# Q and K of the next batch inside the attention loop, 64x64 score matmuls with a plain maximum, and GpSimd sums cut into tiles

## The reference

```
xn = layernorm(x)
q, k, v = xn @ Wq + bq, xn @ Wk + bk, xn @ Wv + bv    # 16 heads of 16
# blocks of 64 rows; a block's queries see the 192 keys of the blocks
# before, at and behind it, within a band |i - j| <= 64 and inside the sequence
scores = where(mask, einsum(q, k) / sqrt(16), -1e9)
a = softmax(scores) @ v @ Wo + bo
h = layer_norm(a + xn) * g1 + b1
f = gelu(h @ W1 + c1) @ W2 + c2                       # 256 -> 1024 -> 256
attn = layer_norm(f + h) * g2 + b2
e = argmax(xn @ gate_w.T)                             # one expert of 8 per token
ffn = xn + xn @ expert_w[e].T
out = x + attn + ffn
```

## Time and profile before

| | us |
|---|---|
| median of 3 runs | 1558.98 |
| lowest and highest | 1557.52, 1561.96 |
| span of the profiled execution | 1553.1 |
| TensorE matmul busy | 1240.9 (80%) |
| VectorE busy | 1071.5 (69%) |
| ScalarE busy | 739.8 (48%) |
| GpSimd busy | 739.9 (48%) |

### The profile page before, as it was taken

How to read it: one execution, slowest core, us unless ns; L and a number is a source line. 1 busy time by engine, 2 the same in 40 slices (tenths; PEclk the granted TensorE clock), 3 DMA queues, 4 the chain that set the end, 5 groups by cost and what they waited for, 6 DMA issues and landing times.

```text
span 1553.1 us, 34323 instructions
## 1 busy us (share of the span) xinstructions
PE 1240.9 (80%) x10696; PEld 714.8 (46%) x10696; DVE 1071.5 (69%) x3743; ACT 739.8 (48%) x1356; POOL 739.9 (48%) x749
## 2 busy tenths in 40 slices
PE   0648885999678985999859997689858898599967
PEld 0424452735346353654527454373535535265435
DVE  8656775777757775867757677576766676587565
ACT  1305744366543744447443565426544374445642
POOL 6443745156531766037550474406752177504661
PEclk9959997999989997989979899798988899799979
DMA  7463056220733119130462206422082212912010
GB/s 237 92 139 118 3 117 122 76 92 29 144 79 100 57 69 166 50 112 13 108 131 69 99 8 145 91 83 83 33 156 75 88 57 74 162 48 94 2 28 28
DMA packets 89647, 135.00 MB, mean 87 GB/s; under 512 B 10209, under 2 KB 62305, under 8 KB 87393
## 3 DMA queue, kind: packets, MB, share of 16 engines
q1 hardware_dynamic: 83328, 115.91, 30.0%
q0 software_dynamic: 6144, 16.79, 4.4%
HBM read 74.47 MB, written 59.90 MB: 87 GB/s over the span
## 4 chain that ended last, share of the span: by engine, by line
PE 49%; DMA 17%; issue 11%; POOL 8%; DVE 8%; SPq 3%; ACT 3%; DVEq 0%; POOLq 0%; ACTq 0%
DMA pair_dram<-pool 9%; PE bank L1132 8%; PE bank L1035 8%; PE bank L1154 8%; PE bank L1036 7%; PE bank L1038 7%; PE bank L1181 6%; DMA q_s<-q_s 5%; DVE xn L604 2%; SPq L284 2%; DMA ys_dram<-xn 2%; PE bank L1102 2%; POOL x_sb L453 2%; POOL x_sb L451 2%; POOL rs L386 2%
## 5 line engine op out<-in xcount | busy, mean ns | idle before, releaser
L713 DVE CUSTOM_DVE_ANT_0 bank<-bank,mask 128x192 f32<-128x192 f32 x1024 | 337.3, 388 | 199.1 <-PE bank L1132 195.1
L943 ACT ACTIVATE pool<-bank 128x512 f32<-128x512 f32 x512 | 293.0, 597 | 118.9 <-PE bank L1154 113.2
L1132 PE MATMUL bank<-k_s,q_s 128*64 128x192 f16 x2048 | 175.3, 269 | 144.1 <-DMA q_s<-q_s 141.2
L440 POOL TENSOR_SCALAR_AFFINE_SELECT pool<-pool 128x512 f32<-128x512 f32 x256 | 172.2, 675 | 194.1 <-ACT pool L943 193.4
L1154 PE MATMUL bank<-q_s,k_s 128*128 128x256 f16 x1024 | 199.3, 290 | 28.7 <-issue 21.3
L389 POOL TENSOR_TENSOR rs<-ve,neghalf 128x1 f32<-128x1 f32 x64 | 36.9, 577 | 384.8 <-DVE ve L776 384.8
L1132 PEld LDWEIGHTS bank<-k_s,q_s 128*64 128x64 f16 x2048 | 77.8, 113 | 250.1 <-issue 226.9
L1181 PE MATMUL bank<-pool,v_a 128*32 128x256 f32 (+2 forms) x2560 | 161.1, 345 | 19.9 <-DVE pool L727 8.6
L989 ACT ACTIVATE pool<-bank,c1c 128x512 f32<-128x512 f32 x128 | 87.8, 686 | 169.5 <-PE bank L1038 132.5
L790 DVE TENSOR_TENSOR pool<-pool 128x512 f16<-128x512 f32 x128 | 106.7, 839 | 63.3 <-ACT pool L955 62.2
L713 DVE DVE_READ_ACCUMULATOR2_ANT m_sb<- 128x1 f32 x1024 | 144.6, 141 | 0.3
(11 more groups left out here) (149 smaller groups left out, 2511.1 us busy)
## 6 DMA issues: line engine op xcount, KB each, us to landing
pair_dram<-pool SPq DMA_DIRECT2D x32, 512.0 KB, 7.6
xn<-xs_dram SPq DMA_DIRECT2D x40, 384.0 KB, 3.7
ys_dram<-xn SPq DMA_DIRECT2D x120, 128.0 KB, 1.7
q_s<-pair_dram SPq DMA_DIRECT2D x48, 256.0 KB
k_s<-pair_dram SPq DMA_DIRECT2D x48, 256.0 KB
x_sb<-in_L_attn_x SPq DMA_DIRECT2D x8, 1024.0 KB, 5.7
res_dram<-x_sb SPq DMA_DIRECT2D x8, 1024.0 KB, 4.8
res_r<-res_dram SPq DMA_DIRECT2D x8, 1024.0 KB, 7.4
```

Of the source, the lines that this page charges most:

```text
L440: nc.gpsimd.affine_select(out=p, in_=p, compare_op=ALU.is_ge, fill=0.0, base=0, pattern=[[0, 4], [1, 2 * W]], channel_multiplier=-1).then_ ...
L713: ins = nc.vector.tensor_tensor_reduce(out=SB[u % 2][:, i * WIN:i * WIN + WIN], in0=SB[u % 2][:, i * WIN:i * WIN + WIN], in1=mask[:, v, :] ...
L943: nc.scalar.activation(prob[:, (k + 2) % 3, 2 * pu:2 * pu + 2, :], TB[u % 2][:, :].rearrange("p (h q) -> p h q", h=2), ACT.Exp, scale=EXP_ ...
L1132: mm = nc.tensor.matmul(SB[u % 2][W * bl:W * bl + W, i * WIN:i * WIN + WIN], q_s[:, h, W + w0:2 * W + w0], k_s[:, h // 2, w0:w0 + WIN], st ...
```

## The change

Seven things change.

- Q and K of the next batch are computed in thirds (two matmuls each) within steps 18 to 29 of the attention loop, two thirds a step, over the two banks of `MB` instead of four banks. For that the norm moves ahead: statistics in steps 0 to 8, `xn` from step 10, its transposes from step 14. x is loaded one turn earlier, within the sorted tiles of the turn before.
- The columns of Wq and Wk are permuted on the way in, so that a head's 16 channels lie eight partitions apart; stores go to `pair_dram` slot by slot (12 of 256 KB instead of 4 of 512 KB), and loads fill 48 partitions at once (8 of 384 KB instead of 12 of 256 KB and two small ones).
- Plain scores: eight matmuls of 48 rows by 64 stationary columns, heads of the two partition halves into different banks, and four matmuls with an identity that add the mask in PSUM; both halves in one block. VectorE then takes two reductions over 2 x 192 instead of four instructions with a mask and four reads.
- The maxima's transpose uses a bank of `SB`; TensorE waits for it before the next scores of that step.
- Transposed scores keep their shape; the two halves of a step are grouped by partition half and are not split by plain scores.
- VectorE's factor of the second norm moves behind two tiles of V.
- GpSimd's sums over eight tiles become eight sums of one tile each.

```
-    XN_AT = 23
+    XN_AT = T + 2
+    XT_AT = XN_AT + 4
+    QK_AT = XT_AT + 4
-        QB, VB = TB + MB, OB + TB
+        QB, VB = MB, OB + TB
...
+            def pair_stores(b, i):
+                c, qk = divmod(i, 2)
+                for src, done, slots in ((qk_h, qk_hi, (0, 2 if qk else 1)), (qk_l, qk_lo, (1 if qk else 2,))):
+                    sp.wait_ge(done.sem, done.at(b, 2 * i + 2))
+                    for slot in slots:
+                        sp.dma_start(pair_dram[c, qk, :, :, slot, :, :].rearrange("j a d s -> d (j a) s"),
+                                     src[:, 2 * qk + c, :]).then_inc(pair_st[i % 2].sem, 16)
+            def stack_loads(b, i, first=False):
+                c, qk = divmod(i, 2)
+                if not first and qk == 0:
+                    sp.wait_ge(ST_ps.sem, ST_ps.at(b - 1, 4 * T * (c + 1)))
+                sp.wait_ge(pair_st[i % 2].sem, pair_st[i % 2].at(b, 48 * (i // 2 + 1)))
+                for a in range(2):
+                    dst = k_s[:, 4 * c:4 * c + 4, :] if qk else q_s[:, 8 * c + a:8 * c + 8:2, :]
+                    sp.dma_start(dst[W * a:W * a + KW, :, W:W + S],
+                                 pair_dram[c, qk, :, a, :, :, :].rearrange("j o d s -> (o d) j s")).then_inc(stack[c].sem, 16)
...
+                    if i == 10 and x_next:                      # sorted_tiles, SP
+                        load_x(b + 1)
             def turn(b, last):                                  # SP
                 max_rows(b, 1)
-                if not last:
-                    load_x(b + 1)
                 load_res(b)
-                for g in range(2, G):
-                    max_rows(b, g)
-                if not last:
-                    store_res(b + 1)
-                    stacks(b + 1)
+                max_rows(b, 2)
+                max_rows(b, 3)
+                if not last:
+                    # pair_stores 0, 1; stack_loads 0, 1; pair_stores 2, 3; stack_loads 2, 3
+                    store_res(b + 1)
                     sorted_tiles(b + 1)
...
-                nc.gpsimd.tensor_tensor(res_r[:, :, :], res_r[:, :, :], x_sb[:, :, :], ALU.add).then_inc(res_y.sem, 1)
+                for t in range(T):
+                    nc.gpsimd.tensor_tensor(res_r[:, t, :], res_r[:, t, :], x_sb[:, t, :], ALU.add).then_inc(res_y.sem, 1)
...                                                              # likewise the other five sums
+            def qk_low(b, u):                                   # VectorE
+                dve.wait_ge(qk_hi.sem, qk_hi.at(b, u + 1))
+                nc.vector.scalar_tensor_tensor(out=qk_l[:, o, s], in0=QB[u % 2][:, :], scalar=bqk[:, o:o + 1],
+                                               in1=qk_h[:, o, s], op0=ALU.add, op1=ALU.subtract).then_inc(qk_lo.sem, 1)
...
             def c2_stage(b, first=False):                       # VectorE
-                if not first:
-                    nm1_stage(b - 1)
                 for t in range(T):
+                    if t == 2 and not first:
+                        nm1_stage(b - 1)
...
             def maxima(b, j):
+                for n, par in enumerate((1, 0)):
+                    dve.wait_ge(S_ps.sem, S_ps.at(b, 2 * j + n + 1))
-                        ins = nc.vector.tensor_tensor_reduce(
-                            out=SB[u % 2][:, i * WIN:i * WIN + WIN], in0=SB[u % 2][:, i * WIN:i * WIN + WIN], in1=mask[:, v, :], scale=1.0,
-                            scalar=-3.0e38, op0=ALU.add, op1=ALU.max, accum_out=m_sb[:, h, t:t + 1])
+                    nc.vector.tensor_reduce(m_sb[:, 4 * g + par:4 * g + 4:2, t],
+                                            SB[par][:, 0:2 * WIN].rearrange("p (h c) -> p h c", h=2), AX.X, ALU.max).then_inc(mx.sem, 1)
...
             def turn(b, last):                                  # VectorE
-                    if k == 2 * T + MAX_AT and not last:
+                    if k < T and not last:
+                        c1_tile(b + 1, k)
+                    if k == T and not last:
                         c1_stage(b + 1)
+                    if XT_AT <= k < XT_AT + 4 and not last:
+                        xn_low(b + 1, k - XT_AT)
+                    if QK_AT <= k < QK_AT + 12 and not last:
+                        for third in range(2 * (k - QK_AT), 2 * (k - QK_AT) + 2):
+                            if third % 3 == 2:
+                                qk_low(b + 1, third // 3)
...                                                              # ScalarE: qk_high at the same places
+            def qk_third(b, u, part):                           # TensorE
+                o, hf = u % 4 // 2 * 2 + u // 4, u % 2
+                dst = QB[u % 2][:, :]
+                if part == 0:
+                    if u >= 2:
+                        pe.wait_ge(qk_lo.sem, qk_lo.at(b, u - 1))
+                    else:
+                        pe.wait_ge(xT_l.sem, xT_l.at(b, 4))
+                # two matmuls of 512 columns; the third part ends with .then_inc(qk_ps.sem, 1)
+            def score_mm(out, n, j, par, i):
+                h, r = 2 * g + i, slice(W * par, W * par + KW)
+                q = W + (2 * t + n) * W
+                return nc.tensor.matmul(out[W * n:W * n + W, i * WIN:i * WIN + WIN], q_s[r, 2 * h + par, q:q + W], k_s[r, h, q - W:q + 2 * W],
+                                        start=i == 0, stop=False, skip_group_check=True)
+            def mask_mm(out, n, t, par):
+                r = slice(W * par, W * par + W)
+                band = mask[r, edge(2 * t + n), :, :].unsqueeze(1).broadcast_to([W, 2, 2, W])
+                dst = out[W * n:W * n + W, 0:2 * WIN].rearrange("p (h c k) -> p h c k", h=2, c=3)[:, :, 0::2, :]
+                return nc.tensor.matmul(dst, ident16[r, :], band, start=False, stop=True, skip_group_check=True)
+            def scores(b, j, first=False):
+                for par in (1, 0):
+                    scores_wait(b, j, par, first)    # mx of step j - 1 for this half; mT_ev in MAX_STEPS
+                for i in range(2):
+                    for n in range(2):
+                        for par in (1, 0):
+                            score_mm(SB[par], n, j, par, i)
+                for n in range(2):
+                    for par in (1, 0):
+                        mm = mask_mm(SB[par], n, t, par)
+                        if n == 1:
+                            mm.then_inc(S_ps.sem, 1)
+            def max_cols(b, g, issued):
+                pe.wait_ge(mx.sem, mx.at(b, 2 * issued))
+                nc.tensor.transpose(SB[g % 2][0:4 * T, 0:P], m_sb[:, 4 * g:4 * g + 4, :].rearrange("p h t -> p (h t)"),
+                                    ident[:, :]).then_inc(mT_ps.sem, 1)
             def turn(b, last):                                  # TensorE
                 for k in range(STEPS + LAG):
                     if k % T == MAX_AT and k < 3 * T:
-                        max_cols(b, k // T + 1)
-                    for pu in range(2):
+                        max_cols(b, k // T + 1, min(k - 1 + LEAD, STEPS))
+                    for par in range(2):
                         if k < STEPS:
-                            scores_t(b, k, pu)
-                        if 1 <= k and k - 1 + LEAD < STEPS:
-                            scores(b, k - 1 + LEAD, half=pu)
+                            scores_t(b, k, par)
+                        if QK_AT <= k < QK_AT + 12 and not last:
+                            qk_third(b + 1, *divmod(2 * (k - QK_AT) + par, 3))
+                    if 1 <= k and k - 1 + LEAD < STEPS:
+                        scores(b, k - 1 + LEAD)
+                    if XT_AT <= k < XT_AT + 4 and not last:
+                        xn_transposes(b + 1, k - XT_AT)
                     if k >= LAG:
                         values(b, k - LAG)
```

More of the change, by code:

```diff
@@ L87, in build @@
     assert len(W1_STEPS) + T == LEAD
+    MAX_STEPS = [LEAD - T + 3] + [T * g + MAX_AT - 1 + LEAD for g in range(G - 2)]
     def tiles_at(t):
@@ L365, in _ @@
             sorted_tiles(0)
[L366 removed]
+            with sp.Fori(0, NB - 2) as b:
                 turn(b, False)
+            turn(NB - 2, False, x_next=False)
             turn(NB - 1, True)
@@ L499, in turn @@
                     band(b, k)
-                    if k == XN_AT - 1 and not last:
+                    if k == T and not last:
                         rstd(b + 1, 0, ve0, rs0)
@@ L848, in _ @@
             assert done == N_PREP_Z
+            for t in range(T):
+                c1_tile(0, t)
             c1_stage(0)
@@ L854, in _ @@
                 xn_low(0, u)
+            for u in range(8):
+                qk_low(0, u)
             dve.wait_ge(pprep.sem, N_PPREP_V)
@@ L1003, in _ @@
                 xn_high(0, u)
-            c2_stage(0)
+            for u in range(8):
+                qk_high(0, u)
             weights_b()
@@ L1048, in xn_transposes @@
                 pe.wait_ge(xn_rdy.sem, xn_rdy.at(b, TH * (u // DC) + TH))
-                if u == 0 and not first:
```

(7 more changed lines are left out.)

261 lines of the change are left out of this document (129 added, 132 removed).

## The result

The changed kernel takes 1516.9 us (median of 4 runs, 1514.0 to 1521.5), the kernel before 1559.6 beside it: ratio 0.9727, 95% interval 0.9708 to 0.9747, 2.7% faster. The forecast was 1479, 5.1% faster. The profiled execution's span is 1511.9 us.

What follows compares the result with a forecast made beforehand. Bound before: TensorE work plus one stack DMA wait per turn; after, GpSimd's chain. 1553.1 + 2 (first part) - 8 (last turn) - 7 x 10.6 (turns 182.6 to 172) = 1472.9, plus 5.9 around the span: 1479 us; range 1418 to 1550.

Steps and rivals of the forecast that it cites:

- The first tile: Arrival of the first sorted tile at the end of GpSimd's chain: S + 125.4, 8 us after W1.
- step, block, reduction: Attention loop: step 1.8 us, set by the TensorE-VectorE handshake; score and mask block 0.39; reductions 0.50, second with tail 0.58.
- handshake hidden: Rival 1, attention loop: steps 1.5 us, no extras, 8 us less per turn, 1422 us; chance 0.15.
- Row tiles don't run side by side: Rival 2, plain score blocks: 0.26 us more in each of 18 steps and 14 blocks outside, 1512 us; chance 0.12.
- The Q and K step: The 12 loop steps holding thirds of Q and K: 1.98 us each on TensorE.
- the loop: Attention loop's end, L = S + 66.4 against S + 55.4 before; bounds 60 and 75.
- Tile sums: GpSimd's chain behind the loop: one tile's sum 0.63 us, bounds 0.56 and 0.75.
- The landing: Landing of GpSimd's eight fetches before its next sums: 2.5 us, bounds 1.9 and 12.1.
- The residual's store: Store on SP's queue that the fetch waits for: done at S + 90, taking 170 GB/s.
- rivals 3 and 4: Residual's store late, fetch S + 96, 1521 us, chance 0.12; stacks at 120 GB/s, fetch S + 107, 1598 us, chance 0.09.
- VectorE waits for all: Start of the tile loop: wait for all 16 MLP sums, ending at 128.6, plus TensorE's lower-clock restart; 2 us added.
- the last turn: Last turn, without Q or K: tile sums beside the gelu save 9 us, the loop costs 1 more; 8 less.

Runs made afterwards that it cites:

- e10: The changed kernel, unedited, timed again in the same batch as e7, e9 and e11: 0.9689 of the kernel before, 1505.9 us.
- e0: The changed kernel, unedited, timed again in the same batch as e5, e6 and e8: 0.9723 of the kernel before.
- e4: Changed kernel with each plain maximum taken over the first 96 of 192 keys, halving the reduction: 0.9504 of the kernel before.
- e9: e11 with Q and K behind the output projection and the residual's store ahead of the stacks' on SP's queue: 0.9447 of the kernel before, 1464.6 us.
- e11: Changed kernel with VectorE waiting for each MLP sum and each residual sum where it uses them: 0.9583 of the kernel before.
- e1: Kernel before with only its six GpSimd sums cut into single tiles: 0.9831 of the kernel before.
- e7: Kernel before with the change's scores only (64x64 blocks, TensorE mask, plain reductions, transposed scores, maxima's transpose in SB): 1.0134 of the kernel before.
- e6: Changed kernel with Q and K behind the output projection and the residual's store ahead of the stacks' on SP's queue: 0.9610 of the kernel before.
- e2: Changed kernel with GpSimd's six sums over all eight tiles again: 0.9957 of the kernel before.
- e5: Changed kernel with VectorE's waits tile by tile and GpSimd's eight sends ahead of the residual's sums: 0.9706 of the kernel before.
- e8: e9 with GpSimd's eight sends ahead of the wait for the fetch and the residual's sums: 0.9679 of the kernel before.

## Why the prediction was right or wrong

**Right: the bound, where ScalarE has no unnamed waits.** The chain from root to sorted rows took the stack wait's place: in e10 every turn waits for the sorted rows. The end of W1 is close behind it. In the turn shown it comes 0.3 us before them, and in e0, with 54.3 us of unnamed waits on ScalarE, it is the bound. The first tile was forecast for S + 125.4 and came at S + 127.0.

**Right: step, block, reduction.** Forecast 1.8, 0.39, 0.50 and 0.58; measured 1.79, 0.40, 0.47 apart and 0.55 each. TensorE alone needs 1.59 (e4) and not 1.5, because the transposed scores take 0.61 and not 0.54. Of the rivals, "handshake hidden" falls with e4, which shows what a hidden one is worth: a turn of 172.3, so 3 to 4 us and not the 8 of the rival. "Row tiles don't run side by side" falls with the 0.40. The Q and K step was 1.98, as forecast.

**Mis-sized: the loop, L = S + 68.8 for 66.4.** The term that was missing is the loop's start. The sum counts step 0 and all that follow at 1.8 us, the price at the full clock, and has nothing for the lower clock behind the turnaround, where TensorE is idle. By that sum step 5 starts at S + 9.0; it starts at 503.57, S + 11.8, 2.8 us later (505.37 in the timeline of TensorE above is step 6). The first ten microseconds of the loop (columns as in the earlier trace rows):

```profile
491.78:496.78 5.00, 3.73 (x24) 1.47 (x24) 1.37 (x3) 3.26 (x6) 2.50 (x5) 0.50 0.53 179
496.78:501.78 5.00, 4.45 (x46) 1.74 (x47) 3.20 (x8) 1.08 (x2) 2.39 (x4) 0.56 0.00 2
```

The turn from which the forecast took its rows is, up to the root, the shortest of the six middle turns of the kernel before; its clock is back at 0.97 in the second five microseconds, that of the next turn at 0.61:

```profile
504.01:509.01 5.00, 5.00 (x59) 1.85 (x57) 3.92 (x23) 3.05 (x6) 3.00 (x5) 0.97 0.02 5
684.72:689.72 5.00, 5.00 (x41) 1.52 (x39) 2.80 (x15) 2.17 (x4) 2.45 (x4) 0.61 0.01 3
```

The rest of the loop came nearly as worked out. Steps 5 to 17 took 27.8 us for 28.3, and this holds the 1.83 us for which TensorE idles before 518.03, where a maxima transpose waits for VectorE amid the norm, and the lower clock behind it until 521. Steps 18 to 29 took 24.7 for 24.2, the end 4.5 for 4.9.

**Right on balance, by errors that cancel: root to first tile.** Tile sums: 0.69 each for the forecast's 0.63, and 0.93 beside VectorE (7.40 for 8). Eight fetches 11.5 for 10.1, sends 10.0 for 10.7, from the last send to the first tile 4.8 for 7. The landing was 1.9 for 2.5. The residual's store, priced at S + 90 with 170 GB/s, was issued at 571.39 (S + 79.6) and lands in 6.1 by the page: the fetch never waited for it, and rivals 3 and 4 did not come. Their DMA rate came from a stretch of the old stack loads, 120 GB/s at a share of 1.08; in the kernel after the engines move 233 GB/s at a share of 0.99 from 560 to 575, where the second half of the new stacks is loaded. The landing of 1.9 goes with stacks that are on their way before the fetch; in e9, where both fall together, it is 5.8.

**Mis-sized: what follows the first tile.** Its term was "VectorE waits for all", and 2 us for that and the lower clock. The two sets of eight sums took 11.9 and not 10.2, from a start 3.8 later, and ended at S + 134.2 and not 128.6; the tile loop took 46.8 us where 42.9 (2 of it this) was forecast, the turnaround 4.0 for 3.3. e11 shows the wait by itself: without it the stretch from W1 to the next loop is 2.4 us shorter than in e10.

**Mis-sized: the last turn,** of which 8 us were forecast, 9 gained with the gelu less 1 for the loop; 2.8 came (139.4 to 136.6). The 9 are nearly right: from W1's start to the end it is 53.6 us and was 62.0, and e1, with the tile sums alone, has 53.5. The loop's term is what failed: from the table load to W1's start it is 83.0 us and was 77.5, 5.5 more where 1 was forecast, and e7, with the scores alone, has 82.5. The start of the last turn's loop, first the kernel before (the clock is 1.00 in the five microseconds behind this row too), then the kernel after:

```profile
1415.60:1420.60 5.00, 4.94 (x54) 1.99 (x55) 4.16 (x25) 3.96 (x7) 3.80 (x7) 1.00 0.61 210
```

```profile
1377.32:1382.32 5.00, 4.54 (x44) 1.79 (x44) 2.20 (x6) 2.69 (x6) 3.62 (x6) 0.61 0.61 210
1382.32:1387.32 5.00, 4.41 (x46) 1.72 (x45) 1.79 (x5) 2.00 (x4) 1.32 (x3) 0.50 0.03 7
```

The kernel before ran here at the full clock, the kernel after did not. The wait for the last of GpSimd's sums, 1.0 us a tile here beside a busy VectorE, costs this turn 1.6 us at most (from W1's start 53.5 in e10, 51.9 in e11).

**The sum.** 4.6 us a turn (176.6 for 172) are 32.2, the last turn 5.2, the first part 1.5 (139.1 for 137.6), less 0.9 around the span: the 38 between 1479 and 1517. The turn shown is 177.8, with 2.4 of its excess in the loop, 3.9 in the tile loop and 0.8 less between them. The range was not what its words say: half way from 1479 to rival 4's 1598 is 1538, not 1550.

**Wrong in attribution.** The forecast let the 15.6 us of Q and K and the 17.1 of the wait fall together, as the gain of moving Q and K. By e6 and e9 the wait falls without that move, with the new stacks; and Q and K in the loop make it end 7 us later and start GpSimd's chain late by as much, where behind the loop they run beside that chain. The forecast knew that the chain was the bound and that it hangs on the loop's end; it did not draw the conclusion that TensorE work is then best placed behind the loop. That its time came within the range owes something to luck: it gave to one part of the change what another brought.

## What to carry to other kernels

When a serial chain on one engine bounds a turn, look where it starts: here the other engines' work belonged behind that point, not before it (1.1 and 1.4 points, e6 and e9), since filling idle slots ahead of it delays the bound. A wait for the last of eight pieces gives back part of what splitting into eight gained, and splitting the wait as well brought 1.1 points here. A stage that starts behind an idle stretch wants a price at the lower clock. And a change of several parts wants each part undone or done alone: here one part alone is a loss (+1.3%), one a gain (-1.7%), and the largest wait went without the move of Q and K that was meant to remove it.

## What the runs showed of the hardware

- A GpSimd sum of 128x2048 fp32 takes 4.5 us, and VectorE instructions of 0.2 to 0.7 us beside it took 4.5 to 5.3 (e2). In eight pieces the sum takes 5.5 alone and 6.4 to 8.7 beside VectorE, and VectorE's gelu part lasts 0.85 in the mean (108.1 us for 128 in the kernel after) where 0.69 is its time alone. (The Trainium skill, SBUF — State Buffer, Who interferes with whom, has the second of the two wait for the first's whole instruction where VectorE reads two inputs from SBUF; e1 and e2 agree, with 0.68 and 4.46 for the same one.)
- ScalarE and VectorE sometimes waited, up to 6.5 us, for what TensorE had, by the records, finished; the waits looked at began while GpSimd issued its indirect DMAs. They were seen in the first trace of the changed kernel and in the four of one batch (e0, e5, e6, e8), and in none of the kernel before and of the eight of the other two batches. Their cause is open.
- Twelve matmuls in 64x64 tiles (eight of 192 columns, four of 256) took 0.40 us from the first start to the start of what follows, at the full clock.
